# A DLRM tower in fp32 on one Trainium2 core: the places of TensorE's waits are changed

## The chip, the cores and the metric

The kernel runs on one core of a Trainium2 chip. The metric is device time in microseconds (us) of one execution. The engines are TensorE (PE, with its weight loads shown apart as PEld), VectorE (DVE), ScalarE (ACT), GpSimd (POOL) and SyncE (SP), which here only starts DMAs. Each engine runs its own list of instructions in order; between engines there are only semaphores.

## What is computed

2048 samples. Each has 26 ids, one per embedding table (128 numbers a row), and a dense vector of 128. The 27 vectors of a sample are multiplied pairwise (351 products), the dense vector is put behind them, and three layers follow.

```python
combined = jnp.concatenate([sparse_x, dense_x[:, None, :]], axis=1)      # 2048 x 27 x 128
interact = jnp.einsum('bfd,bgd->bfg', combined, combined)
z = interact[:, _TRIU_I, _TRIU_J]                                        # 2048 x 351
h = jnp.concatenate([z, r_dense_x], axis=1)                              # 2048 x 479
h = jnp.maximum(h @ W_top1 + b_top1, 0.0)                                # 512
h = jnp.maximum(h @ W_top2 + b_top2, 0.0)                                # 256
y = h @ W_top3                                                           # 1
```

## The kernel before, in words

The samples are 16 tiles of 128, two tiles are a chunk, so there are 8 chunks (c = 0 to 7). Every engine's order is written out by hand.

**Features.** Sixteen of the tables are gathered by POOL: one indirect DMA for each table and tile (L303, 256 in all) into one of two buffers `rows`; PE transposes them by groups of four (`turn`, L661) and ACT copies each group into `xt` (`evac_group`, L479). The ten small tables (1000 rows) are looked up by matmul: DVE makes a one-hot matrix in eight units of 128 table rows (`make_units`, L345, semaphore `s_unit`), and PE multiplies each unit with the high and the low part of the table (`lookup(e)`, L650, 16 matmuls of 512 columns for one table and four tiles). There are 41 such steps e: 8 in chunk 0, 5 in each of chunks 1 to 6, 3 in chunk 7. PE reports every second unit as used, and DVE then writes that place for the next step. ACT copies the result of a step into `xt` (`evac(e)`, L458, semaphore `s_lk`). The dense vectors are copied by ACT too (`evac_dense`, L474, `s_xdense`).

**Pairs.** `gram(n, part)` (L677) takes half a tile: 64 small matmuls in the source, each two loads and two matmuls in the trace, so 128 of each. A finished tile is transposed out of `ps_gram` by DVE (`pack`, L364, `s_zs`), packed, turned by PE (`turn_pairs`, L691) and copied into `zt` by ACT (`evac_zt`).

**Layers.** `layer1(m, j)` (L707) is four products for a fourth of the hidden units of chunk m: k = 0, 1, 2 over the pairs and k = 3 (NZ) over the dense vector, which is loaded into the last part of `zt` by SP (`s_densez`); each product is two loads and two matmuls in the trace. `relu1` (L492) follows on ACT, `layer2(m, t)` (L714) on PE, `finish` (L388, L390, `s_y`) on DVE.

**PE's order in chunk c = 2 to 6** (with a = 2c and f the first step of the next chunk) is: turn, lookup(e+3), turn_pairs, lookup(e+4), layer1(c-1,0), gram(a,0), lookup(f), turn, layer1(c-1,1), turn, layer1(c-1,2), gram(a,1), turn, layer1(c-1,3), turn, lookup(f+1), layer2(c-1,0), gram(a+1,0), turn, lookup(f+2), turn, gram(a+1,1), turn, turn_pairs, layer2(c-1,1). Chunk 7 has fewer lookups, and behind it stand the last two tiles' layers (L727, L737, L744).

The waits that the change touches all stand on PE. In chunks 1 to 7 `lookup` waits for units in two halves of four. `gram(n, 0)` waits for its tile's groups (`s_turned`), the dense columns (`s_xdense`) and the transpose of the tile before (`s_zs`). `layer1(m, 0)` waits for the pairs (`s_zt`), the dense part (`s_densez`) and the last results (`s_y`), and ahead of its product k = 3 for the last lookup of the next chunk's features (`s_lk`).

Of the kernel before, what the change touches and what calls it, by code (L numbers as in the profile page):

```python
# [17 lines left out]
TILES = B // P  # L18
# [9 lines left out]
KT = 8  # L28
# [5 lines left out]
CT = 2  # L34
# [8 lines left out]
STEP0 = []  # L43
# [54 lines left out]
USE = 2  # L98
# [14 lines left out]
def build(nc, t_, out):  # L113
    ctx = ExitStack()
    with ctx:
# [6 lines left out]
        def sem(name):  # L122
            return ctx.enter_context(nc.semaphore(name))
# [40 lines left out]
        s_densez = sem("s_densez")  # L164
# [12 lines left out]
        s_unit = sem("s_unit")  # L177
        s_unit_used = sem("s_unit_used")
        s_tr = sem("s_tr")
        s_lk = sem("s_lk")  # L180
        s_turned = sem("s_turned")
        s_xdense = sem("s_xdense")
        s_gpart = sem("s_gpart")
        s_zero = sem("s_zero")
        s_zs = sem("s_zs")
# [13 lines left out]
        def slot(n):  # L199
            a = n % XT * P  # L200
            return slice(a, a + P)

        def split_count(j):
            return FIRST_PARTS + j
# [3 lines left out]
        def lookup_bank(e):  # L208
            return ps_mlp if e == SPARE else ps_lk[(e if e < SPARE else e - 1) % LB]

        def mlp_bank(n):
            return (ps_mlp, ps_zt)[n % 2]

        def layer2_bank(t):
            return (ps_zt, ps_mlp)[t]
# [412 lines left out]
        def _(pe):  # L628
# [4 lines left out]
            def lookup(e, ks=range(KT)):  # L633
                c, w, tables = STEPS[e]
                for k in ks:
                    if c == 0:
                        pe.wait_ge(s_unit, e * KT + k + 1)
                    elif k % (KT // 2) == 0:
                        pe.wait_ge(s_unit, e * KT + k + KT // 2)
                    if e == 0 and k % (KT // FIRST_PARTS) == 0:  # L640
                        pe.wait_ge(s_low, k // (KT // FIRST_PARTS) + 1)
                    if 0 < e < STEP0[1] and k == 0:
                        pe.wait_ge(s_low, split_count(tables[-1]))
                    if e >= LB and e != SPARE and k == 0:
                        pe.wait_ge(s_lk, e - LB if SPARE < e <= SPARE + LB else e - LB + 1)
                    for j, i in enumerate(tables):
                        x = slice(j * w * P, (j + 1) * w * P)
                        for part in range(2):

                            m = nc.tensor.matmul(lookup_bank(e)[:, x], table[:, i, part, k, :], onehot[:, k, x],  # L650
                                                 start=(k == 0 and j == 0 and part == 0),
                                                 stop=(k == KT - 1 and part == 1), skip_group_check=True)
                    if k % USE == USE - 1:
                        m.then_inc(s_unit_used, 1)
# [9 lines left out]
            def gram(n, part):  # L664
                if part == 0:
                    pe.wait_ge(s_turned, (n + 1) * NGR)
                    if n == 0:
                        pe.wait_ge(s_lk, STEP0[1])
                    pe.wait_ge(s_xdense, n // CT + 1)
                    if n > 0:  # L670
                        pe.wait_ge(s_zs, n)
                    else:
                        pe.wait_ge(s_zero, 1)
                for s in range(part * (Q // PARTS), (part + 1) * (Q // PARTS)):
                    for q in range(QUADS):
                        x = slot(n).start + q * Q + s
                        i = nc.tensor.matmul(ps_gram[q * Q:q * Q + GS, s, 0:GS], xt[:, x, 0:GS],  # L677
                                             xt[:, x, 1:NF], start=True, stop=True)
                i.then_inc(s_gpart, 1)
# [14 lines left out]
            def layer1(m, j):  # L694
                if j == 0:
                    pe.wait_ge(s_zt, m * CT + CT)
                    pe.wait_ge(s_densez, m * 16 + 16)
                if j >= 2:
                    pe.wait_ge(s_act, m * T1 + j - 1)
                elif j == 0 and m > 0:  # L700
                    pe.wait_ge(s_y, m * CT)
                for k in range(NZ + 1):
                    r = ZT[k][1] if k < NZ else D
                    if j == 0 and k == NZ:

                        pe.wait_ge(s_lk, STEP0[m + 2])
                    i = nc.tensor.matmul(mlp_bank(j)[:, 0:CS], w1[0:r, k, j * P:(j + 1) * P], zt[0:r, k, :],  # L707
                                         start=(k == 0), stop=(k == NZ))
                i.then_inc(s_mlp, 1)

            def layer2(m, t):
                pe.wait_ge(s_act, m * T1 + T1)
                for k in range(T1):
                    i = nc.tensor.matmul(layer2_bank(t)[:, 0:H2], h1[:, k, t * P:(t + 1) * P], w2[:, k, :],  # L714
                                         start=(k == 0), stop=(k == T1 - 1))
                i.then_inc(s_mlp, 1)
# [33 lines left out]
            pe.wait_ge(s_ident, 2)  # L750
            warm_up()
            lookup(0)
            turn(0, 0)
            lookup(1)
            lookup(2)
            turn(0, 1)
            lookup(3)
# [7 lines left out]
            e = STEP0[1]  # L765
            lookup(e)
            gram(0, 0)
            turn(1, 1)
            lookup(e + 1)
            turn(1, 2)  # L770
            gram(0, 1)
            lookup(e + 2, range(0, KT // 2))
            turn(1, 3)
            lookup(e + 2, range(KT // 2, KT))
            gram(1, 0)
            turn_pairs(0)
            turn(2, 0)
# [5 lines left out]
            for c in range(1, CHUNKS - 1):  # L783
                a, e, f = c * CT, STEP0[c], STEP0[c + 1]
                if c == 1:
                    turn(a, 2)
                    lookup(e + 4)
                    turn_pairs(a - 1)
                    turn(a, 3)
                    lookup(f)  # L790
                    pe.wait_ge(s_cols, 16)
                    pe.wait_ge(s_base, 2)
                    pe.wait_ge(s_w, 16 * 4)
                    pe.wait_ge(s_lk, SPARE + 1)
                    layer1(c - 1, 0)
                    gram(a, 0)
                else:
                    turn(a, 3)
                    lookup(e + 3)
                    turn_pairs(a - 1)  # L800
                    lookup(e + 4)
                    layer1(c - 1, 0)
                    gram(a, 0)
                    lookup(f)
                turn(a + 1, 0)
                layer1(c - 1, 1)
                turn(a + 1, 1)
                layer1(c - 1, 2)
# [3 lines left out]
                turn(a + 1, 3)  # L812
                lookup(f + 1)
                layer2(c - 1, 0)
                gram(a + 1, 0)
                turn(a + 2, 0)
# [3 lines left out]
                turn(a + 2, 2)  # L820
                turn_pairs(a)
                layer2(c - 1, 1)


# [10 lines left out]
            layer1(c - 1, 3)  # L835
            turn(a + 1, 2)
            layer2(c - 1, 0)
            layer2(c - 1, 1)
            turn_pairs(a)
# [62 lines left out]
```

## Time and profile before

| | |
|---|---|
| time, median of 3 runs | 360.32 us (357.79 to 360.86) |
| the profiled execution, its own time | 359.57 us |
| its span in the profile | 357.8 us |
| PE busy | 334.9 us, 94% of the span |
| PEld busy | 276.7 us, 77% |
| POOL busy | 249.4 us, 70% |
| DVE busy | 237.9 us, 66% |
| ACT busy | 178.9 us, 50% |

What lies between span and time is 1.7 us. In the rows "idle before X <- Y" means that the engine stood idle ahead of work X and that Y ended that; "issue" means that nothing the profile shows was waited for. PE's matmuls overlap one another and their ends are modelled, so the starts of the weight loads (PEld) show stalls more sharply than PE's busy share.

### The profile page before, as it was taken

Reading aid. Unit: us, or ns where it says so; the run is one execution under the profiler, and the core shown is the slowest. Engines: PE = TensorE matmul, PEld = TensorE weight load, DVE = VectorE, ACT = ScalarE, POOL = GpSimd, SP = SyncE. Lnnn points to the kernel's source line nnn. Section 1 sums busy time; section 2 is a strip of 40 time slices with the busy share of each in tenths; the row PEclk is TensorE's granted clock in tenths of the full one; section 3 lists DMA queues with packets and bytes.
Section 4 is the critical chain, followed back from the end, with each engine's and each line's share of the span. In section 5 each row is a group of like instructions: output and inputs, shape, how many; then the busy total and the mean of one; then the engine's idle time right before and its main releaser. Section 6 shows DMA issues by size and latency. Waiting matters only on the chain.

```text
span 357.8 us, 12483 instructions
## 1 busy us (share of the span) xinstructions
PE 334.9 (94%) x5572; PEld 276.7 (77%) x5572; DVE 237.9 (66%) x440; ACT 178.9 (50%) x238; POOL 249.4 (70%) x265
## 2 busy tenths in 40 slices
PE   8999999998897999999999989999999999988976
PEld 8788878777676788877888768787888788867775
DVE  5899979846666757778378864787587793430422
ACT  4888554645246443473627625176344836363222
POOL 6778777777777777777777777777777777777000
PEclk9999999999999999999999999999999999999999
DMA  7998773332333334434243233333333322222000
GB/s 232 384 248 233 182 239 94 105 99 53 97 93 81 90 91 102 100 79 116 64 118 84 83 101 96 89 83 83 97 98 94 88 53 63 60 55 57 21 5 1
DMA packets 19657, 37.67 MB, mean 105 GB/s; under 512 B 5557, under 2 KB 8501, under 8 KB 19604
## 3 DMA queue, kind: packets, MB, share of 16 engines
q1 hardware_dynamic: 11412, 20.09, 20.1%
q0 software_dynamic: 8192, 16.79, 18.1%
q8 instruction: 44, 0.72, 0.8%
q14 instruction: 9, 0.07, 0.1%
HBM read 36.85 MB, written 0.01 MB: 103 GB/s over the span
## 4 chain that ended last, share of the span: by engine, by line
PE 62%; POOL 13%; DVE 12%; issue 8%; DMA 3%; ACT 1%; DVEq 0%
PE ps_lk L650 24%; POOL rows L303 13%; PE ps_gram L677 11%; DVE onehot L345 10%; PE ps_tr L661 6%; PE ps_mlp L707 6%; PE ps_zt L707 6%; PE ps_zt L714 3%; PE ps_mlp L714 2%; DMA rows<-in_tbl,gather_ids 2%; DVE table L356 2%; PE ps_lk L727 1%; PE ps_zt L691 1%; ACT xt L479 1%; DMA gather_ids<-in_ids_gather 1%
## 5 line engine op out<-in xcount | busy, mean ns | idle before, releaser
L303 POOL DMA_INDIRECT rows<-in_tbl,gather_ids x256 | 248.0, 969 | 80.2 <-issue 75.3
L345 DVE TENSOR_SCALAR onehot<-ids 128x513 fp32r<-128x513 f32 (+3 forms) x328 | 178.8, 616 | 50.0 <-PE ps_lk L650 32.8
L650 PE MATMUL ps_lk<-onehot,table 128*128 128x512 f32 (+1 forms) x704 | 156.1, 374 | 1.7 <-DVE onehot L345 1.1
L650 PEld LDWEIGHTS ps_lk<-onehot,table 128*128 128x128 f32 x704 | 118.5, 188 | 25.4 <-DVE onehot L345 4.4
L479 ACT COPY xt<-ps_tr 128x512 f32<-128x512 f32 x64 | 77.3, 1208 | 103.3 <-PE ps_tr L661 103.3
L677 PEld LDWEIGHTS ps_gram<-xt 128*26 128x26 f32 x4096 | 43.9, 103 | 20.8 <-issue 17.4
L677 PE MATMUL ps_gram<-xt 128*26 128x26 f32 x4096 | 53.2, 192 | 6.1 <-issue 2.6
L364 DVE STREAM_TRANSPOSE zs<-ps_gram 128x832 f32<-128x832 f32 x16 | 16.8, 1050 | 50.8 <-PE ps_gram L677 50.8
L661 PE MATMUL ps_tr<-ident,rows 128*128 128x128 f32 x256 | 39.7, 278 | 6.4 <-DMA rows<-in_tbl,gather_ids 5.7
L458 ACT COPY xt<-ps_lk 128x512 f32<-128x512 f32 x31 | 37.0, 1235 | 10.8 <-PE ps_lk L650 6.3
L661 PEld LDWEIGHTS ps_tr<-ident,rows 128*128 128x128 f32 x256 | 29.4, 140 | 13.2 <-DMA rows<-in_tbl,gather_ids 7.0
L450 ACT ACTIVATE ids<-ids,first 128x516 f32<-128x516 int32 (+3 forms) x41 | 29.0, 707 | 2.1 <-DMA ids<-in_ids_first 1.7
L707 PE MATMUL ps_mlp<-zt,w 128*128 128x256 f32 (+1 forms) x112 | 27.8, 385 | 0.4 <-DVE y L390 0.4
L707 PE MATMUL ps_zt<-zt,w 128*128 128x256 f32 (+1 forms) x112 | 26.7, 381 | 0.0
L707 PEld LDWEIGHTS ps_mlp<-zt,w 128*128 128x128 f32 (+1 forms) x112 | 20.3, 190 | 4.9 <-ACT xt L458 1.8
L707 PEld LDWEIGHTS ps_zt<-zt,w 128*128 128x128 f32 (+1 forms) x112 | 20.2, 191 | 2.2
L485 ACT COPY zt<-ps_zt 128x256 f32<-128x256 f32 x16 | 5.9, 371 | 17.7 <-PE ps_zt L691 17.7
L714 PE MATMUL ps_zt<-w,h 128*128 128x256 f32 x56 | 13.3, 381 | 0.1
L714 PE MATMUL ps_mlp<-w,h 128*128 128x256 f32 x56 | 13.2, 380 | 0.0
L492 ACT ACTIVATE h<-ps_mlp,cols 128x256 f32<-128x256 f32 x14 | 6.6, 473 | 11.7 <-PE ps_mlp L707 11.7
L492 ACT ACTIVATE h<-ps_zt,cols 128x256 f32<-128x256 f32 x14 | 6.6, 474 | 10.6 <-PE ps_zt L707 10.6
L714 PEld LDWEIGHTS ps_zt<-w,h 128*128 128x128 f32 x56 | 10.5, 189 | 1.9 <-ACT h L492 0.4
(65 smaller groups left out, 153.2 us busy)
## 6 DMA issues: line engine op xcount, KB each, us to landing
ids<-in_ids_onehot SPq DMA_DIRECT2D x40, 258.0 KB, 3.6
rows<-in_tbl,gather_ids POOLq DMA_INDIRECT x256
w<-in_tbl SPq DMA_DIRECT2D x6, 512.0 KB, 6.9
h<-in_tbl SPq DMA_DIRECT2D x2, 512.0 KB, 6.0
zt<-in_tbl SPq DMA_DIRECT2D x2, 512.0 KB, 5.8
dense_x<-in_dense SPq DMA_DIRECT2D x8, 128.0 KB, 3.7
zt<-in_dense SPq DMA_DIRECT2D x8, 128.0 KB, 2.4
w<-in_w SPq DMA_DIRECT2D x1, 512.0 KB
```

What stands on the lines that cost most here:

```text
L303: pool.indirect_dma_start(rows[n % ROW_BUFS][:, r, :], None, t_[f"tbl_{GATHERED[r]}"], bass.IndirectOffsetOnAxis(ap=gather_ids[:, n, r:r + ...
L345: nc.vector.tensor_scalar(to, of.bitcast(F32), float(k), None, ALU.is_equal).then_inc(s_unit, 1)
L364: nc.vector.transpose(zs[:, :, :], ps_gram[:, :, 0:GS].rearrange("p s g -> p g s")).then_inc(s_zs, 1)
L450: nc.scalar.activation(ids[e % IDS][:, 0:w].bitcast(F32), ids[e % IDS][:, 0:w], ACT.Identity, bias=first[:, :]).then_inc(s_from, 1)
L458: nc.scalar.copy(xt[:, :, a], lookup_bank(e)[:, :]).then_inc(s_lk, 1)
L479: nc.scalar.copy(xt[:, slot(n), a:a + w].rearrange("p s f -> p f s"), ps_tr[:, 0:w * P].rearrange("p (f s) -> p f s", f=w)).then_inc(s_tur ...
L492: nc.scalar.activation(h1[:, j, :], mlp_bank(j)[:, 0:CS], ACT.Relu, bias=cols[:, j:j + 1]).then_inc(s_act, 1)
L650: m = nc.tensor.matmul(lookup_bank(e)[:, x], table[:, i, part, k, :], onehot[:, k, x], start=(k == 0 and j == 0 and part == 0), stop=(k == ...
L661: i = nc.tensor.transpose(ps_tr[:, k * P:(k + 1) * P], rows[n % ROW_BUFS][:, r, :], ident[:, :])
L677: i = nc.tensor.matmul(ps_gram[q * Q:q * Q + GS, s, 0:GS], xt[:, x, 0:GS], xt[:, x, 1:NF], start=True, stop=True)
L707: i = nc.tensor.matmul(mlp_bank(j)[:, 0:CS], w1[0:r, k, j * P:(j + 1) * P], zt[0:r, k, :], start=(k == 0), stop=(k == NZ))
L714: i = nc.tensor.matmul(layer2_bank(t)[:, 0:H2], h1[:, k, t * P:(t + 1) * P], w2[:, k, :], start=(k == 0), stop=(k == T1 - 1))
```

## The change

No instruction that computes or moves data is added, removed or moved; the lists of DVE, ACT, POOL and SP are the same. On PE four things change:

1. In chunks 1 to 7 a lookup waits for units two by two (`USE` = 2) and not four by four.
2. `gram(n, 0)` for n = 1 and 15 still waits for `s_zs`, for n = 2 to 14 no longer; only n = 0 waits for `s_xdense`.
3. `layer1(m, 0)` waits for `s_xdense` at k = 1, for `s_lk` at k = 2 (before: at k = 3) and for `s_densez` at k = 3 (before: at k = 0).
4. `layer2(m, 0)` waits at k = 1 for the `s_zs` that the second gram of the chunk needs.

```diff
-                    elif k % (KT // 2) == 0:
-                        pe.wait_ge(s_unit, e * KT + k + KT // 2)
+                    elif k % USE == 0:
+                        pe.wait_ge(s_unit, e * KT + k + USE)
...
-                    pe.wait_ge(s_xdense, n // CT + 1)
-                    if n > 0:
+                    if n == 0:
+                        pe.wait_ge(s_xdense, 1)
+                        pe.wait_ge(s_zero, 1)
+                    elif n == 1 or n == TILES - 1:
                         pe.wait_ge(s_zs, n)
-                    else:
-                        pe.wait_ge(s_zero, 1)
...
                 if j == 0:
                     pe.wait_ge(s_zt, m * CT + CT)
-                    pe.wait_ge(s_densez, m * 16 + 16)
...
+                    if j == 0 and k == 1:
+                        pe.wait_ge(s_xdense, m + 2)
+                    if j == 0 and k == 2:
+                        pe.wait_ge(s_lk, STEP0[m + 2])
                     if j == 0 and k == NZ:
-
-                        pe.wait_ge(s_lk, STEP0[m + 2])
+                        pe.wait_ge(s_densez, m * 16 + 16)
...
                 for k in range(T1):
+                    if t == 0 and k == 1:
+
+                        pe.wait_ge(s_zs, (m + 1) * CT + 1)
```

PE's list in chunk 2, from lookup(e+4) to the first gram of the chunk, before. The names in brackets are the semaphores that an instruction stands on, and one row of L650 is one matmul of one load:

```order
L650 MATMUL ps_lk<-onehot,table 128x512 [waits s_lk,s_unit]
L650 MATMUL ps_lk<-onehot,table 128x512 x7
L650 MATMUL ps_lk<-onehot,table 128x512 [waits s_unit]
L650 MATMUL ps_lk<-onehot,table 128x512 x7
L707 MATMUL ps_mlp<-zt,w 128x256 [waits s_y,s_densez,s_zt]
L707 MATMUL ps_mlp<-zt,w 128x256 x2
L707 MATMUL ps_mlp<-zt,w 128x256 [waits s_lk]
L677 MATMUL ps_gram<-xt 26x26 [waits s_zs,s_xdense,s_turned]
L677 MATMUL ps_gram<-xt 26x26 x63
```

The same stretch of PE's list now (layer 1 is line 709 there):

```order
L650 MATMUL ps_lk<-onehot,table 128x512 [waits s_unit]
L650 MATMUL ps_lk<-onehot,table 128x512 x3
L650 MATMUL ps_lk<-onehot,table 128x512 [waits s_unit]
L650 MATMUL ps_lk<-onehot,table 128x512 x3
L709 MATMUL ps_mlp<-zt,w 128x256 [waits s_y,s_zt]
L709 MATMUL ps_mlp<-zt,w 128x256 [waits s_xdense]
L709 MATMUL ps_mlp<-zt,w 128x256 [waits s_lk]
L709 MATMUL ps_mlp<-zt,w 128x256 [waits s_densez]
L677 MATMUL ps_gram<-xt 26x26 [waits s_turned]
L677 MATMUL ps_gram<-xt 26x26 x63
```

No instruction moved; the wait for units is at every fourth matmul, the wait for the lookup's copy (`s_lk`) is one product earlier, and the gram has one wait of its three left.

PE's list at the second gram of the same chunk, behind layer2, before:

```order
L714 MATMUL ps_zt<-w,h 128x256 [waits s_act]
L714 MATMUL ps_zt<-w,h 128x256 x3
L677 MATMUL ps_gram<-xt 26x26 [waits s_zs,s_xdense,s_turned]
L677 MATMUL ps_gram<-xt 26x26 x63
L661 MATMUL ps_tr<-ident,rows 128x128 [waits s_turned,s_rows0_0]
```

and now:

```order
L719 MATMUL ps_zt<-w,h 128x256 [waits s_act]
L719 MATMUL ps_zt<-w,h 128x256 [waits s_zs]
L719 MATMUL ps_zt<-w,h 128x256 x2
L677 MATMUL ps_gram<-xt 26x26 [waits s_turned]
L677 MATMUL ps_gram<-xt 26x26 x63
```

Here the wait for the neighbour's transpose stands on the second matmul of layer2, and the gram's other two waits are gone from it.

## Rows read from the trace of the kernel before

**Rows 1.** The page: busy time by engine, and the granted clock in 40 slices.

```profile
PE 334.9 (94%) x5572; PEld 276.7 (77%) x5572; DVE 237.9 (66%) x440; ACT 178.9 (50%) x238; POOL 249.4 (70%) x265
...
PEclk9999999999999999999999999999999999999999
```

**Rows 2.** Weight loads, 86 to 112 us: start, duration, line, count, idle before and its releaser.

```profile
91.07 0.42 PEld L661 LDWEIGHTS ps_tr<-ident,rows 128*128 128x128 f32 x4 [2.97 <-DMA rows<-in_tbl,gather_ids]
...
110.62 0.42 PEld L661 LDWEIGHTS ps_tr<-ident,rows 128*128 128x128 f32 x4 [2.44 <-DMA rows<-in_tbl,gather_ids]
```

**Rows 3.** Waits of POOL (45 to 335 us): us in total, times, longest.

```profile
POOL rows L303 <- issue: 67.1, 220, 0.3
POOL rows L303 <- PE ps_gram L677: 3.3, 7, 1.1
POOL rows L303 <- PE ps_lk L650: 0.3, 1, 0.3
```

**Rows 4.** Waits of the weight loads, 110 to 358 us.

```profile
PEld ps_gram L677 <- issue: 13.1, 45, 1.6
PEld ps_tr L661 <- DMA rows<-in_tbl,gather_ids: 2.4, 1, 2.4
PEld ps_lk L650 <- DVE onehot L345: 2.4, 5, 0.5
...
PEld ps_mlp L707 <- ACT xt L458: 1.8, 5, 0.4
```

**Rows 5.** All engines, 190 to 236 us: lookup(e+4) of chunk 4, layer 1, gram.

```profile
195.46 4.85 DVE L345 TENSOR_SCALAR onehot<-ids 128x513 fp32r<-128x513 f32 x8 [0.43 <-PE ps_lk L650]
...
198.18 1.70 PEld L650 LDWEIGHTS ps_lk<-onehot,table 128*128 128x128 f32 x8
...
200.36 1.70 PEld L650 LDWEIGHTS ps_lk<-onehot,table 128*128 128x128 f32 x8 [0.49 <-DVE onehot L345]
...
202.11 1.28 PEld L707 LDWEIGHTS ps_mlp<-zt,w 128*128 128x128 f32 x6
...
202.53 1.17 ACT L458 COPY xt<-ps_lk 128x512 f32<-128x512 f32 x1 [0.89 <-PE ps_lk L650]
...
203.75 0.30 PEld L707 LDWEIGHTS ps_mlp<-zt,w 128*128 128x128 f32 x2 [0.36 <-ACT xt L458]
...
204.38 1.10 PEld L677 LDWEIGHTS ps_gram<-xt 128*26 128x26 f32 x108 [0.33 <-issue]
```

**Rows 6.** The same answer: two grams without and with waits, a lookup, a layer.

```profile
215.93 1.26 PEld L677 LDWEIGHTS ps_gram<-xt 128*26 128x26 f32 x112 [0.33 <-issue]
...
217.93 1.05 DVE L364 STREAM_TRANSPOSE zs<-ps_gram 128x832 f32<-128x832 f32 x1 [4.11 <-PE ps_gram L677]
...
218.05 1.60 PEld L707 LDWEIGHTS ps_zt<-zt,w 128*128 128x128 f32 x8
...
220.22 3.54 PEld L650 LDWEIGHTS ps_lk<-onehot,table 128*128 128x128 f32 x16
...
225.85 1.33 PEld L677 LDWEIGHTS ps_gram<-xt 128*26 128x26 f32 x118 [0.33 <-issue]
```

**Rows 7.** Weight loads in chunk 0, 13 to 21 us: two lookups, a wait at every unit.

```profile
13.75 7.23 PEld L650 LDWEIGHTS ps_lk<-onehot,table 128*128 128x128 f32 x32
```

**Rows 8.** Waits of the matmuls, 111 to 358 us.

```profile
PE ps_gram L677 <- issue: 2.6, 3, 1.5
PE ps_tr L744 <- issue: 1.6, 1, 1.6
PE ps_zt L691 <- issue: 0.9, 1, 0.9
```

**Rows 9.** The page: the DMA queue of the instructions.

```profile
q8 instruction: 44, 0.72, 0.8%
```

**Rows 10.** Weight loads, 312 to 332 us: two late starts and what lies between.

```profile
316.44 0.27 PEld L691 LDWEIGHTS ps_zt<-ident,packed 128*128 128x128 f32 x2 [1.04 <-issue]
316.66 1.59 PEld L714 LDWEIGHTS ps_mlp<-w,h 128*128 128x128 f32 x8
318.28 0.49 PEld L691 LDWEIGHTS ps_zt<-ident,packed 128*128 128x128 f32 x3
318.72 0.47 PEld L661 LDWEIGHTS ps_tr<-ident,rows 128*128 128x128 f32 x4
319.83 1.60 PEld L707 LDWEIGHTS ps_mlp<-zt,w 128*128 128x128 f32 x8 [0.65 <-ACT zt L487]
321.76 1.16 PEld L677 LDWEIGHTS ps_gram<-xt 128*26 128x26 f32 x101 [0.33 <-issue]
323.85 0.29 PEld L677 LDWEIGHTS ps_gram<-xt 128*26 128x26 f32 x27 [0.93 <-issue]
```

**Rows 11.** All engines, 342 to 358 us: the end of the last gram.

```profile
346.73 0.39 DVE L372 COPY_PREDICATED packed<-lower,zs 128x169 f32<-128x169 int32 x1
347.22 0.73 PEld L744 LDWEIGHTS ps_tr<-w,h 128*128 128x128 f32 x4 [1.76 <-issue]
...
347.98 0.49 PEld L691 LDWEIGHTS ps_zt<-ident,packed 128*128 128x128 f32 x3
```

## The prediction

> **What bounds the kernel now.** I read the page first: PE is busy 94% of the span, at a granted clock of nine tenths or more in every slice, so it stays at the upper level of 2.4 GHz and no stall here has cost it the clock [rows 1]. A full engine only bounds the end if nobody holds it, so next came the waits. In the first third PE does wait: twice a transpose stands for rows that POOL is still gathering, 2.97 us at 91.07 and 2.44 us at 110.62 [rows 2]. POOL itself never stands still there: between 45 and 335 us 220 of its 228 gaps are its own 0.3 us between two gathers, and PE held it only 7 times, 3.3 us with the usual gap in it, so about 1.2 us beyond it [rows 3]. So up to 110.6 us the gathers set the time, and whatever PE gains or loses there is taken up by the wait at 110.62. Behind it not one transpose waits for rows (the 2.4 us of the next table are that very wait) [rows 4], so from 110.6 to the end the time is PE's own list, plus the places where that list stands. These places are what the change can touch.
>
> **The lookup's halves.** Behind 110 us the weight loads stood 5 times for the one-hot units, 2.4 us in total, 0.5 at most [rows 4]. All five are the second half of lookup(e+4), one in each of chunks 2 to 6. In chunk 4 the eight units take DVE 4.85 us from 195.46, 0.606 each: the sixth is ready at 199.10, the eighth at 200.31. PE begins the first half at 198.18 and stands until 200.36 for the eighth [rows 5]. With waits by pairs the third pair needs only the sixth unit, ready long before PE gets there. A lookup without a stall has 16 loads in 3.54 us, so (3.54 - 0.19)/15 = 0.223 us a load [rows 6]; its ninth load would start at 198.18 + 8 x 0.223 = 199.96 and the thirteenth at 200.86, after the eighth unit. The gain is 200.36 - 199.96 = 0.40 us by this, 0.49 by the idle time in the row; I take 0.43. **Five times: -2.15 us.** Nothing turns up in its place: the slack of the last pair is 0.5 us. The other lookups of these chunks find their units ready. Stalls of this kind in chunks 0 to 2 lie ahead of the row wait and give nothing.
>
> **The lookup's copy, one product earlier.** Straight behind lookup(e+4) stands layer1(c-1,0), and the wait for ACT's copy of that very lookup (`s_lk`). In chunk 4 six loads (k = 0 to 2) run from 202.11, then PE idles 0.36 us until the copy is done (202.53 + 1.17 = 203.70), and only the two loads of k = 3 come behind it, at 203.75 [rows 5]. With the wait at k = 2 the same copy releases four loads, so the gram behind it starts two loads later, while the two that ran ahead of the wait no longer do. A layer's eight loads take 1.60 us [rows 6], 0.20 to 0.22 us a load, so this is 0.40 to 0.44 us, I take 0.43. It happens wherever the copy was already late at k = 3: 5 times, 1.8 us in total [rows 4], the same five chunks. **Five times: +2.15 us.** Since the lookup ends 0.43 us earlier, the copy does too, and the gram starts where it did. The two edits cancel: this is the heart of my forecast.
>
> **The gram's waits.** The waits taken from the gram were satisfied long before. What they cost by standing there is seen by comparison: gram(a,1) at 215.93 has no wait and idles 0.33 us before its first load, gram(a+1,0) at 225.85 has all three and idles 0.33 us too [rows 6]. So 0. The new wait in layer2 is covered as well: the transpose of the neighbour ends at 217.93 + 1.05 = 218.98, and the gram, behind the lookup, comes at 225.85; without that cover it would cost at most 1.05 us. `s_xdense` and `s_densez` are loads and copies that ended a chunk ahead or before the lookup's own copy, in ACT's order.
>
> **Do more waits cost anything?** There are two more in each of 33 lookups. In chunk 0 every unit is waited for already, eight waits a lookup: 32 loads in 7.23 us [rows 7], (7.23 - 0.19)/31 = 0.227 us a load against 0.223 with two waits. The bounds are 0 and 16 x 0.004 = 0.06 us a lookup, of which 28 lie behind 110 us: 0 to 1.8 us. I take 0, because the 32 loads span the passage between two lookups too. The Trainium skill ("TensorE: Matmul & The Clock Gate", section on queue depths) says that TensorE's queue holds 64 and pulls weight loads ahead of running matmuls, which would hide a satisfied wait; by that rule the sum is 0 as well.
>
> **Where the instruction stream runs dry.** Five starts have no releaser: three on grams, 2.6 us, one on L691, 0.9, one on L744, 1.6 [rows 8], 5.1 us in all. The instruction queue brought 44 packets, 0.72 MB [rows 9], and PE has 5572 loads and 5572 matmuls [rows 1], so about 253 instructions a packet. Between the late starts at 316.44 and 323.85 lie 2+8+3+4+8+101 = 126 loads, 252 instructions [rows 10]: one packet. I read these stalls as packets that come late when a gram has eaten the one before (a gram half, 256 instructions, is gone in some 1.8 us). The waits taken off 13 grams were instructions of their own where several stood on one matmul, so each later packet border moves one place further down the list: about 8 by chunk 4, 13 at the end. At 316.44 the border moves from L691 into layer 2, whose loads are slower; 6 loads of 0.2 us come ahead of it and the stall of 0.9 us shrinks by some 0.75. At the end it moves behind the four loads of L744, which then run while DVE packs; L691 then waits for DVE's 346.73 + 0.39 = 347.12 instead of starting at 347.98 [rows 11], some 0.6 us. In chunk 4 two more products lie between the released wait and the gram, up to 0.43 us. These give -1.8 us, but other borders move too and may become late: the bounds are -5.1 us (all gone) and +1.6 for each new one [rows 8]. I take half, **-0.9 us**. The Trainium skill ("Runtime: NRT & Kernel Launch", section on instruction fetch mechanics) says that a sequencer fetches blocks of 256 instructions by itself and that this is mostly hidden; the 5.1 us here disagree with "hidden". By that rule this term would be 0 and the forecast 360.3.
>
> **The sum.** 359.57 - 2.15 + 2.15 + 0 + 0 - 0.9 = 358.7 us for the profiled execution, which was 0.75 us below the median of the runs; against the median 360.32 - 0.9 = **359.4 us**.
>
> **The rivals.** *A, the forecast*, the two edits cancel and packet borders shift: 358.2 to 361.0, chance 0.62. *B, faster*: the later product wait costs nothing because the gram was held by something else, so the 2.15 us of the lookups remain, and the borders give up to 3 us more: 360.32 - 2.15 = 358.2 down to 355.2. For it speaks that the loads of L677 idle 13.1 us in 45 places with no releaser named [rows 4]; against it that the load of k = 3 starts 0.05 us after the copy's end, and the gram right behind [rows 5]. Chance 0.20, of which 0.12 is over 1%. *C, slower*: the borders fall where they hurt. A request for a packet that stands behind the wait for the copy goes out late, and the gram behind it runs dry in each of the five chunks: 5 x 1.0 = +5 us, 365.3. It decides from the third new late packet on (3 x 1.3 = 3.9 us). For it speaks that the late one in chunk 4 (the longest wait of L677 in [rows 8]) stands right behind such a wait; against it that borders move by 13 places only out of 256. Chance 0.08 over 1%; another 0.05 for one or two. *D, no effect*: the gathers hold everything. That would need PE to wait for rows behind 110 us, and it doesn't once. 360.3, chance 0.05.
>
> **Range and chances.** The range reaches from most of B to one or two new late packets: 357.2 to 362.2. About 1% (3.6 us) is what a measurement of this kernel can tell from no change; the three runs span 3.1 us. Faster by over 1%: 0.12 (end of B). Slower by over 1%: 0.08 (C). Within: 0.80.
>
> **What would show it.** In the profile after: no wait of L650 for L345 behind 110 us (2.4 us before); the wait of L707 (now L709) for ACT's copy up from 1.8 to about 4.0 us in the same 5 places; the idle time before a gram still 0.33 us; the gram at 204.38 again 6.2 us behind the start of its lookup at 198.18, and every difference of over 0.5 us to be found in starts with no releaser. I am wrong if the wait before L709 does not grow, if lookups are longer than 3.54 us from their first to last load, or if the transposes wait for rows again.

## The result and the profile after

Twenty runs of each kernel: 359.90 us after the change (358.92 to 361.29), 358.47 us before (356.31 to 361.12). The ratio is 1.0039, with a 95% interval of 1.0020 to 1.0058: 0.4% slower, 1.4 us. Of the three runs that the prediction started from, two (360.32, their median, and 360.86) lay in the upper third of these twenty and one (357.79) in the lower half; the profiled one (359.57) was above 15 of the twenty. The profiled execution after took 359.43 us, with a span of 357.7; so the two profiles are of nearly equal length, and what follows compares them place by place and not by their ends.

The page after, busy time and granted clock (the clock now shows an 8 in two slices; compare [rows 1]):

```profile
PE 335.8 (94%) x5572; PEld 278.6 (78%) x5572; DVE 237.7 (66%) x440; ACT 179.2 (50%) x238; POOL 249.1 (70%) x265
...
PEclk9999999999899999999999999999999999999989
```

The waits of the weight loads after, 110 to 358 us (waiting line and tile, releaser: us in total, times, longest). They answer [rows 4]; layer 1 is now line 709:

```profile
PEld ps_gram L677 <- issue: 13.7, 48, 2.1
PEld ps_mlp L709 <- ACT xt L458: 4.0, 5, 0.8
...
PEld ps_tr L661 <- DMA rows<-in_tbl,gather_ids: 1.6, 1, 1.6
```

No lookup waits for units behind 110 us (2.4 us before), and the wait for the copy grew from 1.8 to 4.0 us, again in five places. Both are what was forecast. The weight loads of chunk 4 after, which answer [rows 5]:

```profile
199.20 3.53 PEld L650 LDWEIGHTS ps_lk<-onehot,table 128*128 128x128 f32 x16
202.78 0.86 PEld L709 LDWEIGHTS ps_mlp<-zt,w 128*128 128x128 f32 x4
204.44 0.73 PEld L709 LDWEIGHTS ps_mlp<-zt,w 95*128 95x128 f32 x4 [0.80 <-ACT xt L458]
205.50 1.02 PEld L677 LDWEIGHTS ps_gram<-xt 128*26 128x26 f32 x106 [0.33 <-issue]
```

The lookup is one piece of 16 loads, then four loads of layer 1 and not six run ahead of the copy, and four and not two come behind it. From the lookup's first load to the gram's it is 6.30 us, and it was 204.38 - 198.18 = 6.20: what the pairs gave, the copy took.

Two stretches of this profile are not in the one of before. At 91.5 us the wait for rows is longer (3.82 us, [rows 2] had 2.97), and the lookup behind it takes 5.09 us for 16 loads in place of 3.54:

```profile
91.50 0.42 PEld L661 LDWEIGHTS ps_tr<-ident,rows 128*128 128x128 f32 x4 [3.82 <-DMA rows<-in_tbl,gather_ids]
91.89 5.09 PEld L650 LDWEIGHTS ps_lk<-onehot,table 128*128 128x128 f32 x16
```

And in the last gram, the loads start, stop after 141 of 256 with no releaser, and go on 2.07 us later; before, all 256 ran through and the start without releaser stood on L744 behind the gram ([rows 11]). The last gram after:

```profile
340.33 1.26 PEld L677 LDWEIGHTS ps_gram<-xt 128*26 128x26 f32 x141 [0.56 <-ACT xt L479]
343.67 1.05 PEld L677 LDWEIGHTS ps_gram<-xt 128*26 128x26 f32 x115 [2.07 <-issue]
```

and before:

```profile
342.42 2.25 PEld L677 LDWEIGHTS ps_gram<-xt 128*26 128x26 f32 x256 [0.55 <-ACT xt L479]
```

TensorE came to this gram 2.1 us earlier than before, and lost all of it behind it. That it was earlier has much to do with one start without releaser that was there before, in the gram of chunk 4 right behind [rows 5], and is not there after (that gram, from 205.50 us, has all its 128 loads done when the next lookup begins at 207.35). The rows before:

```profile
205.67 0.16 PEld L677 LDWEIGHTS ps_gram<-xt 128*26 128x26 f32 x5 [0.19 <-issue]
207.44 0.20 PEld L677 LDWEIGHTS ps_gram<-xt 128*26 128x26 f32 x15 [1.62 <-issue]
```

From the last gram's first load to the end of the span, "the tail" below, it was 357.8 - 342.4 = 15.4 us before and is 357.7 - 340.3 = 17.4 us after. The stretches of the two new places (at 92 us and in the last gram) after (length, busy time of each engine, then granted clock, DMA share, GB/s):

```profile
91.80:97.00 5.20, 5.20 (x19) 4.16 (x18) 2.95 (x5) 1.65 (x2) 3.98 (x5) 0.67 0.17 50
...
343.60:348.10 4.50, 4.43 (x127) 3.93 (x128) 1.96 (x3) 0.00 (x0) 0.00 (x0) 0.65 0.01 4
```

The granted clock is 0.67 and 0.65 there: about 3.4 us at the lower level of 1.2 GHz in the first ((1 - 0.67) x 2 x 5.2). In the profiled execution before it never fell ahead of the last instruction.

### The profile page after: what moved, and what is told of

Read it like the earlier page. It is cut to its first block, busy times and chain, and to the rows that moved or that the text cites. A ratio compares the mean times of both kernels' runs of the same rounds, so it can differ in the third digit from the quotient of the medians.

```text
span 357.7 us, 12469 instructions
## 1 busy us (share of the span) xinstructions
PE 335.8 (94%) x5572; PEld 278.6 (78%) x5572; DVE 237.7 (66%) x440; ACT 179.2 (50%) x238; POOL 249.1 (70%) x265
## 3 DMA queue, kind: packets, MB, share of 16 engines
q0 software_dynamic: 8192, 16.79, 17.4%
## 4 chain that ended last, share of the span: by engine, by line
PE 77%; POOL 7%; issue 5%; DVE 4%; DMA 3%; ACT 3%; DVEq 0%; ACTq 0%
PE ps_lk L650 34%; PE ps_gram L677 13%; PE ps_tr L661 7%; POOL rows L303 7%; PE ps_zt L709 6%; PE ps_mlp L709 6%; PE ps_zt L719 3%; PE ps_mlp L719 3%; DVE onehot L345 3%; DMA rows<-in_tbl,gather_ids 3%; ACT xt L458 2%; PE ps_zt L691 1%; PE ps_lk L732 1%; DVE table L356 1%; PE ps_mlp L650 1%
## 5 line engine op out<-in xcount | busy, mean ns | idle before, releaser
L650 PE MATMUL ps_lk<-onehot,table 128*128 128x512 f32 (+1 forms) x704 | 155.9, 375 | 1.0 <-ACT xt L470 0.7
L650 PEld LDWEIGHTS ps_lk<-onehot,table 128*128 128x128 f32 x704 | 120.0, 190 | 23.0 <-issue 0.9
L661 PE MATMUL ps_tr<-ident,rows 128*128 128x128 f32 x256 | 39.9, 278 | 6.1 <-DMA rows<-in_tbl,gather_ids 5.9
L661 PEld LDWEIGHTS ps_tr<-ident,rows 128*128 128x128 f32 x256 | 29.4, 140 | 14.0 <-DMA rows<-in_tbl,gather_ids 7.5
```

Of the source, the lines that this page charges most:

```text
L661: i = nc.tensor.transpose(ps_tr[:, k * P:(k + 1) * P], rows[n % ROW_BUFS][:, r, :], ident[:, :])
```

## Experiments

Theory T, after the result: the edits on units and on the copy cancel as forecast; what is left is where the instruction packets begin (theory B) and the clock. Rival N: one of the two edits gives or costs nothing. Rival W: the gram's moved waits cost or gain by themselves, not through the packets. A border is the place in TensorE's list at which an instruction packet begins; a late start is one without a releaser that is well over the usual 0.2 to 0.33 us. Each kernel has 11 or 12 timed runs against some 30 of the kernel before on the same chip.

**Part by part.** Pairs alone (`e1`):

```diff
-                    elif k % (KT // 2) == 0:
-                        pe.wait_ge(s_unit, e * KT + k + KT // 2)
+                    elif k % USE == 0:
+                        pe.wait_ge(s_unit, e * KT + k + USE)
```

> Before, with only part 1 of the change: lookups of chunks 1 to 7 wait for units by pairs; all other waits as before. Theory T (two edits cancel, the clock falls once): the five halves of 2.4 us in chunks 2 to 6 go, 2.15 us; the product's wait for the copy stays at 1.8 us in 5 places; but TensorE reaches the row wait near 88 us earlier, as in the changed kernel, the wait grows from 2.97 to 3.8 us, the granted clock falls to 1.2 GHz for 3.4 us and 0.7 us of it lasts: -1.4 us against before, ratio 0.996, mean clock 0.99. Rival R (packet borders do it all): no border moves here, so the full 2.15 us show, ratio 0.994, clock 1.0. Rival N (pairs gain nothing because something else holds the gram): 1.000.

Measured: ratio 0.9953 (0.9921 to 0.9986), -1.7 us. The wait for the copy stays at 1.8 us in 5 places, the units are not waited for. Repeated at the end as `e15`:

> Pairs alone once more, as the measure for the other two on this chip and to see whether it is faster than before again: 0.995, tail 15.5 us. If chance between chips made the first result, it is 0.998 to 1.000.

Measured: 0.9968 (0.9946 to 0.9991). So the pairs gain 1.1 to 1.7 us, less than the 2.15 us of the forecast. The profiles show two things on this. The late start in chunk 4 is gone as well. The loads of that gram in `e1`:

```profile
205.03 0.66 PEld L677 LDWEIGHTS ps_gram<-xt 128*26 128x26 f32 x69 [0.33 <-issue]
205.86 0.56 PEld L677 LDWEIGHTS ps_gram<-xt 128*26 128x26 f32 x53 [0.17 <-issue]
206.62 0.18 PEld L677 LDWEIGHTS ps_gram<-xt 128*26 128x26 f32 x6 [0.19 <-issue]
```

No border moved here: the late start in the tail stands on L744 again. The late start near 208 us is in all three profiles of kernels with halves and the gram's old waits (1.62 us before, 1.34 in `e7`, 1.51 in `e10`), and in none of the others. So waiting by pairs brought one packet in time; how is open. From lookup(e+4) in chunk 2 to that in chunk 6 it is 165.2 and 165.3 us (`e1`, `e15`) and was 167.7: 2.4 to 2.5 us less in four chunks, of which 1.4 is this packet and some 1.1, or 0.3 a chunk, is left for the units, not 0.43. Some of that may turn up again at the transposes (L661 without a releaser, 2.4 to 2.5 us behind 115 us, 2.0 before); this is not shown.

The other half alone, the changed kernel with units by halves (`e2`):

```diff
-                    elif k % USE == 0:
-                        pe.wait_ge(s_unit, e * KT + k + USE)
+                    elif k % (KT // 2) == 0:
+                        pe.wait_ge(s_unit, e * KT + k + KT // 2)
```

> The changed kernel, but lookups wait for units in halves as before; the gram's waits stand on layers 1 and 2. Theory T: the wait for the copy is 4.0 us in 5 places and the halves cost 2.4 us again: +2.15 us against before, ratio 1.006, and since TensorE is not early at 88 us the clock does not fall there (mean 1.0). Rival R (borders): the same borders as the changed kernel, so whatever it loses by them is lost here too, on top: above 1.008. Rival N: 1.000 to 1.002.

Measured: 1.0040 (1.0011 to 1.0070), and in its profile 2.1 us without releaser in the last gram. Against this, the earlier wait for the copy and nothing else, in the kernel before (`e7`):

```diff
-                    if j == 0 and k == NZ:
-
+                    if j == 0 and k == 2:
                         pe.wait_ge(s_lk, STEP0[m + 2])
```

> Before, with one edit: layer 1 waits for s_lk at k = 2 and not at k = 3. Theory T: the wait for the copy grows from 1.8 to 4.0 us in 5 places, +2.15 us, ratio 1.006, no border moves. Rival N (the gram is held by something else): 1.000.

Measured: 1.0018 (0.9995 to 1.0041), +0.7 us with an interval that reaches nothing. Its profile is plainer than its median:

```profile
PEld ps_mlp L706 <- ACT xt L458: 4.0, 5, 0.8
PEld ps_lk L650 <- DVE onehot L345: 2.4, 5, 0.5
```

Between the starts of lookup(e+4) in chunks 2 and 6 lie 284.98 - 115.52 = 169.46 us in this kernel and 282.77 - 115.04 = 167.73 before: 1.73 us for four chunks, 0.43 each, the term of the prediction (both profiles have the late start near 208 us). In the changed kernel it is 281.88 - 115.72 = 166.16, and 166.61 in its second profile (`e5`). Without its late start of 1.4 us beyond the usual, before had 166.3: the two edits cancel to within 0.3 us in four chunks.

The changed kernel with the copy waited for at k = 3 again (`e3`):

```diff
-                    if j == 0 and k == 2:
-                        pe.wait_ge(s_lk, STEP0[m + 2])
-                    if j == 0 and k == NZ:
-                        pe.wait_ge(s_densez, m * 16 + 16)
+                    if j == 0 and k == 2:
+                        pe.wait_ge(s_densez, m * 16 + 16)
+                    if j == 0 and k == NZ:
+                        pe.wait_ge(s_lk, STEP0[m + 2])
```

> The changed kernel, but layer 1 waits for s_lk at k = 3 as before and for s_densez at k = 2. Theory T: the wait for the copy is back at 1.8 us, so 2.15 us faster than the changed kernel, ratio to before 0.998, the clock still falls near 92 us (0.99). Rival R: borders as in the changed kernel, 1.004 if they make the loss and the copy's wait is hidden. Rival N: 1.004.

Measured: 0.9974 (0.9946 to 1.0002), as T says, with a tail of 17.4 us. Two comparisons on this one chip price the two edits in medians: `e4` below, which has the copy at k = 2 and else differs from `e3` only in lookups ahead of the row waits, took 359.94 us against 358.43, so +1.5 us for the copy; `e2`, with halves in all lookups, took 361.21, so 1.3 us for the pairs.

**The clock near 92 us.** I took the fall to come from TensorE's earlier arrival at the row wait. `e4` has halves in steps 8 to 13:

```diff
                     if c == 0:
                         pe.wait_ge(s_unit, e * KT + k + 1)
+                    elif e <= STEP0[2]:
+                        if k % (KT // 2) == 0:
+                            pe.wait_ge(s_unit, e * KT + k + KT // 2)
                     elif k % USE == 0:
```

> The changed kernel, but steps 8 to 13 (all before the row wait near 88 us) wait by halves as before. Theory T: TensorE arrives at the row wait as late as before (idle 3.0 us), the clock stays at 2.4 GHz there, lookup 14 has its loads in 3.54 us again (5.09 in the changed kernel), and some 0.7 us come back: ratio to before 1.002. Rival R: nothing changes against the changed kernel, 1.004, because the loss is in late instruction packets at the end.

The ratio is 1.0007 (0.9981 to 1.0033), but the mechanism is refuted. The loads at the wait:

```profile
91.02 0.42 PEld L664 LDWEIGHTS ps_tr<-ident,rows 128*128 128x128 f32 x4 [2.88 <-DMA rows<-in_tbl,gather_ids]
91.41 5.11 PEld L653 LDWEIGHTS ps_lk<-onehot,table 128*128 128x128 f32 x16
```

The engine idled only 2.88 us, less than before (2.97, with 3.54 us for the same loads), and the clock fell all the same (0.86 between 88 and 100 us). It fell in `e7` too, the kernel before with nothing but the copy's wait moved, behind an idle of 2.95 us; in `e8` it did not fall behind 3.92 us. And most runs of the kernel before have a fall somewhere: of the 31 it has beside these four kernels, 4 have a mean granted clock of 1.00, 21 of about 0.995 (one fall of this length), 6 less. So the fall at 92 us does not belong to the change; the profile of before was one of the few executions without any. What decides it from run to run is open.

**The instruction packets.** First the changed kernel again (`e5`), as the measure for three others on one chip:

> The changed kernel as it is, to stand beside the next three on one chip. Theory T (the two edits cancel and the rest is packet borders): ratio to before 1.001 to 1.004; the wait for the copy 4.0 us in 5 places, a start without releaser of 2.0 us inside the last gram. Rival A (all of it is chance between chips): 0.997 to 1.000.

Measured: 1.0011 (0.9991 to 1.0031), 359.94 us. That is less above before than in the twenty runs, while its own time is the same to 0.04 us; the intervals overlap. The changed kernel with the gram's old waits kept beside the new ones (`e6`):

```diff
                     if n == 0:
                         pe.wait_ge(s_lk, STEP0[1])
-                    if n == 0:
-                        pe.wait_ge(s_xdense, 1)
-                        pe.wait_ge(s_zero, 1)
-                    elif n == 1 or n == TILES - 1:
+                    pe.wait_ge(s_xdense, n // CT + 1)
+                    if n > 0:
                         pe.wait_ge(s_zs, n)
+                    else:
+                        pe.wait_ge(s_zero, 1)
```

> The changed kernel, but the gram keeps its waits for s_xdense and s_zs beside the new ones, so that nearly every instruction packet begins where it began before. Theory B (borders): the 2.0 us inside the last gram go, 1.6 us before L744 and 0.8 us before L691 come back, the mean clock is 0.995 more often than 0.99; ratio 0.5 to 1 us below the changed kernel's, 0.999 to 1.001. [...] Rival 0: no difference.

Measured: 0.9978 (0.9952 to 1.0004), 1.35 us below the changed kernel beside it. More waits, less time: that each wait costs something, one form of rival W, is refuted. It could still be what the waits do. So the next two leave every wait alone and only move the packets, by the count of the warm-up matmuls ahead of all else (each is two loads and two matmuls, 4 instructions: 18 of them are 36 loads and 36 matmuls in the trace). `e9` is the changed kernel with `WARM_UP = 21`, `e10` the kernel before with `WARM_UP = 14`:

```diff
-WARM_UP = 18
+WARM_UP = 21
```

> The changed kernel with 21 warm-up matmuls in place of 18, so 12 instructions more ahead of all else: in the tail the instruction packets begin within 2 places of where they begin before the change. The waits of the change all stay as they are. Theory B (packet borders): the start without releaser inside the last gram (2.0 us) is gone, 1.6 us before L749 is there again, from the last gram's first load to the end 15.4 us and not 17.2; ratio to before 0.998, as with the gram's waits kept. Rival W (what the kept waits did was something else, a cost or an order of TensorE's queue): 1.001 and 17.2 us, as the changed kernel.

```diff
-WARM_UP = 18
+WARM_UP = 14
```

> Before, with 14 warm-up matmuls in place of 18, so 16 instructions fewer ahead of all else: the packets begin 16 places later in the list, as in the changed kernel's tail (14). No wait differs from before. Theory B: a start without releaser of 2.0 us inside the last gram, from its first load to the end 17.2 us, 15.4 in before; the 0.9 us before L691 gone; ratio 1.002 to 1.004. Rival W: 1.000.

Measured: `e9` 0.9984 (0.9960 to 1.0007), `e10` 1.0021 (0.9991 to 1.0050). The last gram's loads in `e9`:

```profile
341.85 2.25 PEld L677 LDWEIGHTS ps_gram<-xt 128*26 128x26 f32 x256 [0.56 <-ACT xt L479]
...
346.20 0.51 PEld L749 LDWEIGHTS ps_tr<-w,h 128*128 128x128 f32 x3 [1.20 <-issue]
```

and in `e10`, the kernel before with four warm-ups fewer:

```profile
342.86 1.28 PEld L677 LDWEIGHTS ps_gram<-xt 128*26 128x26 f32 x142 [0.56 <-ACT xt L479]
346.58 1.04 PEld L677 LDWEIGHTS ps_gram<-xt 128*26 128x26 f32 x114 [2.44 <-issue]
```

The stop after 141 or 142 loads goes with the places of the packets, with every wait as it was: twelve instructions at the very start take it out of the changed kernel, sixteen fewer put it into the kernel before. In time these two are weaker evidence than in the trace: the interval of `e10` holds 1, and that of `e9` overlaps that of `e5`. Then the borders moved the other way, with pairs alone: `e11` has `WARM_UP = 22`, `e12` has `WARM_UP = 28`.

> Lookups by pairs alone, and 22 warm-up matmuls: borders 16 places up the list. Theory B: whatever the time does, it does by starts without releaser; the waits for units and for the copy stay as with pairs alone (0 and 1.8 us behind 110 us). Ratio 0.992 to 1.000, with pairs alone 0.9953. Rival W: 0.995 exactly, since no wait changes.

> The same with 28 warm-up matmuls, borders 40 places up. The first lookup starts some 2 us later, which the row wait near 110 us takes up. Theory B: the border now stands ahead of the last gram's first load, so its two halves eat two packets that were asked for earlier; the time lies between 0.990 and 1.001. Rival W: 0.995.

Measured: `e11` 1.0029 (1.0004 to 1.0054), `e12` 1.0050 (1.0021 to 1.0079); with 18 warm-ups the same kernel has 0.9953 and 0.9968. Both lose all that the pairs gain, and more, and their intervals do not touch those of `e1` and `e15`. Not all of that is in the tail: `e11` has two more late starts in chunk 7 (1.27 us at 315, 1.14 at 323, where `e1` has 0.59 at 315 and 0.76 at 322), `e12` one of 1.34 at 291. The last gram in `e11`:

```profile
341.27 2.24 PEld L677 LDWEIGHTS ps_gram<-xt 128*26 128x26 f32 x254 [0.56 <-ACT xt L479]
345.64 0.13 PEld L677 LDWEIGHTS ps_gram<-xt 128*26 128x26 f32 x2 [2.14 <-issue]
```

Now it is the next border: after 254 loads, and with 142 in `e10` this is 112 loads apart. `e11` has its borders 32 instructions (16 loads) further up than `e10`, so from one border to the next it is 112 + 16 = 128 loads, 256 instructions, one packet. `e12` agrees: 24 instructions more than `e11`, and the stop after 242 loads, 12 earlier. All profiles, by where the late start stands and by the clock (the tail is from the last gram's first load to the end of the span, the granted clock is its mean there, one profile each):

| kernel | late start in the tail | clock | tail, us | ratio to before |
|---|---|---|---|---|
| before | L744, 1.8 us | 1.00 | 15.4 | 1 |
| e1, e15, pairs alone | L744, 1.8 | 1.00 | 15.6, 15.7 | 0.9953, 0.9968 |
| e6, changed, gram's waits kept | L749, 1.5 | 1.00 | 15.2 | 0.9978 |
| e9, changed, borders back | L749, 1.2 | 1.00 | 14.7 | 0.9984 |
| e13, e14 (below) | L743, 1.6; L749, 1.7 | 1.00 | 15.2, 15.3 | 0.9971, 0.9963 |
| e7, copy at k = 2 alone | L743, 1.8 | 0.90 | 17.2 | 1.0018 |
| e8 (below) | L736, 2.2 | 0.90 | 17.5 | 0.9974 |
| e4 | last gram, 2.2 | 0.99 | 16.7 | 1.0007 |
| e10, before, borders moved | last gram, 2.4 | 1.00 | 16.9 | 1.0021 |
| e12, pairs, borders up | last gram, 2.5 | 1.00 | 17.0 | 1.0050 |
| changed (recorded; e5) | last gram, 2.1 | 0.90 | 17.4; 17.1 | 1.0039; 1.0011 |
| e2, e3 | last gram, 2.1 | 0.90 | 17.2, 17.4 | 1.0040, 0.9974 |
| e11, pairs, borders up | last gram, 2.1 | 0.90 | 17.5 | 1.0029 |

Two things lengthen the tail. Where the clock stays up, a late packet behind the gram goes with 14.7 to 15.7 us and one inside it with 16.7 to 17.0: behind the gram DVE is packing and the turn waits for DVE anyway, inside it the stop delays the pack, and all of the last layers stand behind that. Against the 15.4 us of before, the place inside the gram costs 1.3 to 1.6 us. The other thing is the clock. Where it falls behind the stop, the tail is 17.1 to 17.5 us wherever the stop stands. `e7` has the stop of before and a tail 1.8 us longer:

```profile
344.91 2.31 PEld L677 LDWEIGHTS ps_gram<-xt 128*26 128x26 f32 x256 [0.56 <-ACT xt L479]
...
349.83 0.98 PEld L743 LDWEIGHTS ps_tr<-w,h 128*128 128x128 f32 x4 [1.84 <-issue]
...
351.75 1.40 PEld L743 LDWEIGHTS ps_tr<-w,h 128*128 128x128 f32 x4
```

The clock fell there in 5 of 8 profiles with the stop inside the gram and in 2 of 9 with it behind. How often it does so in the other runs is not known: of 12 runs of `e5` 10 have a mean clock of 0.99 or less, of `e9` 5 and of `e6` 3, but the profiles of `e9` and `e6` have 0.99 too, with their tails at the full clock and all of the loss near 92 us. So one profile's tail does not give the median: the ratios in the table follow the tails only roughly.

**Can more be had?** `e8` takes pairs and moves the copy's wait from layer 1 to the gram itself:

```diff
+                    if n >= CT and n % CT == 0:
+                        pe.wait_ge(s_lk, STEP0[n // CT + 1])
                     pe.wait_ge(s_xdense, n // CT + 1)
...
-                    if j == 0 and k == NZ:
-
-                        pe.wait_ge(s_lk, STEP0[m + 2])
```

> Before, with lookups waiting by pairs and the wait for s_lk taken out of layer 1 and put on the gram that needs it. Theory T: the 2.4 us for units and the 1.8 us for the copy both go, -2.15 - 1.7 = -3.85 us, ratio 0.989. Rival N (pairs alone are all there is to gain, since the gram idles 0.33 us before it anyway and then waits itself): -1.7 us as with pairs alone, 0.995. Rival P (TensorE then waits for POOL's rows again): between the two, with waits of L661 for rows behind 115 us.

Measured: 0.9974 (0.9946 to 1.0002), not 0.989. The 1.8 us for the copy are gone from its profile, but a chunk is no shorter than with pairs alone (41.25 us from lookup(e+4) to lookup(e+4) in the last two, 41.2 there). What came instead, its weight loads between 115 and 345 us:

```profile
PEld ps_tr L661 <- issue: 3.5, 5, 1.3
PEld ps_tr L661 <- DMA rows<-in_tbl,gather_ids: 1.0, 1, 1.0
```

One of the five, 1.3 us at 314 us in chunk 7, is a late start between two loads of one transpose group. In chunk 5 the gram starts 5.63 us behind its lookup (5.87 with pairs alone), and at the chunk's end the transpose stands 0.75 us without a releaser (0.43); I take this for ACT's chain of copies, which is not shown. Rival P was half right: TensorE is early enough to meet others. The waits put on the grams had also moved the borders: a late start of 2.2 us stood in the tail, three loads behind the gram, and the clock fell behind it; the tail was 17.5 us long. `e13` is `e8` with `WARM_UP = 16`, `e14` is `e3` with `WARM_UP = 21`:

> The kernel with lookups by pairs and the copy's wait on the gram, and 16 warm-up matmuls in place of 18: the waits put on the grams had moved the borders 6 places up, this moves them 8 down. Theory B (borders): the 2.1 us start before L736 in the tail goes, from the last gram to the end 15.4 us and not 17.5, ratio 0.992 to 0.994. Rival: the copy's wait on the gram costs by itself (0.9974 again).

> The changed kernel with s_lk at k = 3 and 21 warm-up matmuls: the same pairs and copy as with pairs alone, the gram's waits moved, borders back in the tail. Theory B: tail 15.4 us (17.4 with 18 warm-ups), ratio 0.995 as pairs alone. Rival W (moving the gram's waits costs or gains by itself): 0.997 or more, or below 0.993.

Measured: `e13` 0.9971 (0.9947 to 0.9995), tail 15.2 us; `e14` 0.9963 (0.9936 to 0.9991), tail 15.3 us. `e14` stands beside `e15` (0.9968) on one chip: with the borders put back, the kernel with the gram's waits moved and the one without are 0.1 us apart, so those waits by themselves cost or gain at most what these medians can tell, about 1 us. `e13` does not settle how much the copy's wait on the gram gives: its tail became 2.3 us shorter, as expected, and its ratio hardly followed (0.9971 after 0.9974, in two sets of runs). `e3` and `e14`, which differ in the warm-ups alone, are alike: 2.1 us in the tail, 0.4 us in the ratio. One profile a kernel is not enough to say where its other runs lost it. The fastest version stays pairs alone, with nothing else of the change.

## Why the prediction was wrong

**What bounds the kernel: right in the main.** Up to 110 us the gathers: of the stalls for units there (2.0 us in three places) 0.5 in one is left in the changed kernel, and the row waits grew. But the last row wait does not end at a fixed time. It ends between 110.6 and 111.5 us in the four profiles with halves that have it, and between 110.8 and 112.7 in the nine with pairs (110.6 before, 111.3 and 112.0 in the changed kernel). So some of what pairs gain behind it may be lost ahead of it; what moves it is open. Behind it TensorE's list.

**Pairs, -2.15 us: right place, too large.** All five waits went; the runs give -1.7 and -1.1 us. Even that holds a gain that the forecast did not have in this term: the late packet of chunk 4, 1.4 us in the profile.

**The copy, +2.15 us: right in the profile** (4.0 us, 0.43 a chunk in `e7`), +0.7 us in the median of `e7` with an interval up to 1.5. `e9` against `e14`, which differ only in it, have 0.9984 and 0.9963: 0.75 us; `e4` against `e3` is 1.5 us. So the medians have both terms at a third to four fifths of their size, and of opposite sign.

**The gram's waits and more waits, 0: right**, by `e14` and `e15`. The Trainium skill's rule on TensorE's queue ("TensorE: Matmul & The Clock Gate", queue depths), that loads are pulled ahead, fits: a lookup with four waits has its 16 loads in 3.53 us, with two 3.54.

**"Where the instruction stream runs dry", -0.9 us: this step failed.** The mechanism was right, and the runs show it more clearly than I had hoped: borders move with every instruction taken off. But I followed them only at the three stalls I saw (at 207 and 316 us and at L744) and there only for gains. The late start before L691 did go, as forecast, and so did the one in chunk 4, though that one went with the pairs where no border had moved. At L744 I asked what the border leaves when it moves away, and not whether another one, 128 loads ahead, becomes late: the one inside the last gram, which had been in time. It costs +1.3 to +1.6 us at full clock, and +2.0 in the profile of the changed kernel, where the clock fell behind it, and I had -0.6. The whole term, -0.9 in the sum, is +1.0 us (`e5` against `e9`, two chips) to +1.35 us (`e5` against `e6`, one chip). I had called this possible ("+1.6 for each new one") and took half of the gains in place of asking what a move of 14 does to each border in the tail. The -0.6 was also read short: from 347.98 to 347.12 it is 0.86. Rival C named the mechanism, but put it in the five chunks behind the copy's wait, where no packet became late.

With the runs' own numbers the sum is -1.7 to -1.1 (pairs), +0.7 to +1.5 (copy), +1.0 to +1.35 (borders): 0.0 to +1.75 us. Measured were +0.4 (`e5`) and +1.4 us (the recorded comparison). Both lie within, but the sum is no sharper than that: each term is known to about a microsecond.

**The base.** I hung the forecast on the median of three runs, 360.32, because the profiled one stood near. With twenty the median is 358.47. That the changed kernel's 359.9 came within 0.5 us of the forecast 359.4 is luck: from 358.47 the same reasoning gives 357.6, 2.3 us too low. The range holds 359.9 from either base, by its width; the sign was wrong.

## What to carry to other kernels

Where TensorE runs through many short instructions (here 512 in 2.3 us), the place at which an instruction packet begins is a cost of its own: a change that adds or removes a dozen waits far ahead can cost 1 to 2 us at the end, as much as the stalls it was made for. So time such a change once more with a few harmless instructions more or less at the start, before its gain or loss is put down to its idea. And if two waits stand in a row on one path, making the engine stand at the second one instruction sooner gives back what the first gained: look for what stands behind the wait, not only for what it saves.

## What the runs showed of the hardware

- A packet of TensorE's instructions is 256 of them (128 loads and as many matmuls between the stops of `e10` and `e11`, with 32 instructions of shift between the two). The Trainium skill says the same ("Runtime: NRT & Kernel Launch", instruction fetch mechanics), and calls the cost mostly hidden; here a late one of 1.2 to 2.5 us stands in the tail of every kernel profiled.
- At full clock the place of the stop matters more than its length: 1.8 us behind the last gram go with a tail of 15.4 us, 2.2 us inside it with 16.7. With the clock fallen it is 17.2 (`e7`) and 17.1 (`e5`).
- A packet can be late or in time at the same border: in chunk 4 it is 1.62 us late before and in time in `e1`, where lookups wait by pairs.
- The granted clock fell to 1.2 GHz behind an idle stretch of 2.88 us in one kernel (`e4`) and did not behind 2.97 us (before) and 3.92 us (`e8`). Most runs of the kernel before have a mean of 0.995 or less, which its only profile does not show: a single profile of a kernel tells where its time goes in that execution.
